# Two recurrences in one turn, three in the last: a two-pass expert kernel laid out anew from turn 9 on

## What is computed

```
x = x + rwkv(layernorm(x))          # time mix with the WKV recurrence, then channel mix
x = x + experts(layernorm(x))       # 8 experts, top 2, on a batch of tokens
x = x + recurrent(layernorm(x))     # h = a*h + scale*(i*conv(x)); out = rms(h @ W_out) * gamma
x = x + experts(layernorm(x))
# rwkv: k, v, r = mixes of x and its shift times w_key, w_value, w_recept
#       out = wkv(exp(decay), first, k, v) * sigmoid(r) @ w_output; x = x + out
#       vk = square(relu(mix @ f_w_key)) @ f_w_value; x = x + sigmoid(mix @ f_w_recept) * vk
# recurrent: depthwise conv of 4 taps; r, i = sigmoid(conv @ W); a = sigmoid(log_a)**(8*r)
#       scale = sqrt(1 - a*a)
# experts: h = gelu(x[tok] @ w1[e]); y = h @ w2[e]; out[tok] += y * weight, plus bias
```

## Time and profile before

| | us |
|---|---|
| median of three runs | 1547.81 |
| the profiled execution | 1548.36 |
| its span | 1546.6 |
| TensorE busy in it | 1278.7 (83%) |
| VectorE busy | 981.9 (63%) |
| ScalarE busy | 750.1 (48%) |
| GpSimd busy | 666.0 (43%) |

### The profile page before, as it was taken

The page is one execution under the profiler, slowest core; times in us unless marked ns, Lnnn a source line. Parts: engine busy times, 40 slices in busy tenths (PEclk is TensorE's granted clock), DMA queues, the critical chain, the costliest instruction groups (busy, mean ns, idle before and its releaser), DMA issues.

```text
span 1546.6 us, 17067 instructions
## 1 busy us (share of the span) xinstructions
PE 1278.7 (83%) x6050; PEld 1028.8 (67%) x6050; DVE 981.9 (63%) x1476; ACT 750.1 (48%) x1125; POOL 666.0 (43%) x529
## 2 busy tenths in 40 slices
PE   3398688999999999999777777799999989977641
PEld 1275557787778778777656565678778778866531
DVE  6787675557656675766889897956675746132334
ACT  2364254554736455464636363636455463534431
POOL 5323743255362535526565535462435523123161
PEclk9699889999999999999899989899999999998765
DMA  5000033335243333423001000143333425353321
GB/s 159 14 15 1 14 93 129 126 97 166 75 147 114 101 120 122 150 62 93 23 28 41 1 0 27 65 139 121 103 120 122 136 65 170 107 176 97 97 72 41
DMA packets 98372, 137.29 MB, mean 89 GB/s; under 512 B 9000, under 2 KB 83752, under 8 KB 98280
## 3 DMA queue, kind: packets, MB, share of 16 engines
q1 hardware_dynamic: 87408, 119.93, 24.3%
q0 software_dynamic: 4256, 10.24, 2.4%
q10 hardware_dynamic: 6624, 6.03, 1.1%
HBM read 119.64 MB, written 16.54 MB: 88 GB/s over the span
## 4 chain that ended last, share of the span: by engine, by line
PE 56%; DVE 13%; ACT 8%; issue 6%; POOL 4%; DMA 1%; ACTq 0%; POOLq 0%; DVEq 0%
PE psum L905 12%; PE psum L1033 10%; PE psum L1041 9%; PE psum L912 8%; PE psum L989 8%; PE psum L899 6%; PE psum L894 2%; DVE space L1347 2%; POOL xhat L432 1%; ACT dec L641 1%; POOL rstd L428 1%; DVE stats L1217 1%; ACT L792 1%; DVE kc L1308 1%; DVE dec L1310 1%
## 5 line engine op out<-in xcount | busy, mean ns | idle before, releaser
L428 POOL TENSOR_TENSOR rstd<-varis,half_neg 128x4 f32<-128x4 f32 (+1 forms) x48 | 76.8, 1600 | 483.7 <-DVE varis L1232 308.7
L989 PE MATMUL psum<-fwv,hid 128*128 128x256 f32 x1024 | 241.0, 382 | 0.8
L989 PEld LDWEIGHTS psum<-fwv,hid 128*128 128x128 f32 x1024 | 195.9, 192 | 33.7 <-ACT hid L659 3.4
L1033 PEld LDWEIGHTS psum<-xst,ew 128*128 128x128 f32 x1472 | 182.5, 198 | 42.5 <-ACT xst L720 23.5
L1033 PE MATMUL psum<-xst,ew 128*128 128x128 f32 x1472 | 188.1, 283 | 26.1 <-ACT xst L720 18.4
L1041 PE MATMUL psum<-ew,hidt 128*128 128x256 f32 x736 | 169.5, 384 | 4.4 <-ACT hidt L724 4.4
L1041 PEld LDWEIGHTS psum<-ew,hidt 128*128 128x128 f32 x736 | 141.0, 192 | 29.3 <-ACT hidt L724 5.7
L894 PE MATMUL psum<-ident,xhat 128*128 128x128 f32 x384 | 58.4, 302 | 98.8 <-POOL xhat L432 92.2
L894 PEld LDWEIGHTS psum<-ident,xhat 128*128 128x128 f32 x384 | 49.7, 157 | 108.7 <-POOL xhat L432 78.8
L655 ACT ACTIVATE hid<-psum 128x512 f32<-128x512 f32 x128 | 75.3, 597 | 95.3 <-PE psum L905 95.2
L525 POOL DMA_INDIRECT xs<-xf_rows,token_of_slot x46 | 55.8, 1212 | 142.8 <-PE psum L1021 120.3
(11 more groups left out here) (170 smaller groups left out, 2818.0 us busy)
## 6 DMA issues: line engine op xcount, KB each, us to landing
ew<-in_w SPq DMA_DIRECT2D x92, 1024.0 KB, 5.6
rows_ring<-in_x SPq DMA_DIRECT2D x14, 512.0 KB, 5.1
out<-rows_ring SPq DMA_DIRECT2D x14, 512.0 KB, 7.5
ys_rows<-ys ACTq DMA_DIRECT2D x46, 128.0 KB, 4.8
xf_rows<-ew SPq DMA_DIRECT2D x2, 1024.0 KB, 4.4
xf<-in_x SPq DMA_DIRECT2D x2, 512.0 KB, 4.5
space<-in_f_w_key SPq DMA_DIRECT2D x1, 1024.0 KB, 7.5
fwv<-in_f_w_value SPq DMA_DIRECT2D x1, 1024.0 KB, 10.3
```

The costliest lines, as they stand in the source:

```text
L428: pool.tensor_tensor(dst, src, half_neg[:, 0:src.shape[1]], ALU.pow).then_inc(done, 1)
L989: last = nc.tensor.matmul(rows4[:, k, :], hid[:, j % NHID, k * P:(k + 1) * P], fwv[:, j, :], start=j == 0 and k % 2 == 0, stop=j == FC - 1 ...
L1033: last = nc.tensor.matmul(bank_e[:, j * P:(j + 1) * P], ew1[:, c, at:at + P], xst[:, c, :], start=c == 0, stop=c == DC - 1)
```

## The change

`REC_TURN` now says in which turn each place's recurrence runs: places 0 to 5 in turns 4 to 9 as before, 6 and 7 in turn 10, 8 to 12 in turns 11 to 15, and 13, 14 and 15 in turn 16, the last. The turns 9, 10, 11 and 16 have orders of their own on each engine:

- Turn 9 (`turn_ahead`): both batches of pass one are picked and merged (their bias was added in turn 4), and the rows of places 6 and 7 are normalised. The second mix of batch 9 moves from the head of turn 10 to here.
- Turn 10 (`double_turn`): place 6 whole, and place 7 up to its convolution and split.
- Turn 11 (`turn_behind`): place 7 from its gates on, the experts' normalisation of pass two, then place 8 whole, and two tiles of pass two.
- Turns 12 to 15: four tiles each, as turns 13 to 16 had.
- Turn 16 (`tail`): the channel mix of batch 15, places 13 to 15 interleaved, five tiles, then the picks, the merge and the stores. Gated input, scaled input and residual of these places are on VectorE instead of GpSimd, and the last place's power on ScalarE as Ln and Exp.

There are two sets of recurrence buffers, of which the second (places 13 and 15) lies over the time mix's buffers, which are free by then. The scan's output and `fo` lie over `rg`. The normalised rows of place 7 lie in `hidt`, those of place 14 in the second row buffer. Semaphores are split so that steps of two places can be counted apart (`decays_made`, `root`, `gin_b`, `rec_om`), and waits on a shared PSUM bank stand in the order (`freed`) and no longer in the steps. Left out below: renamed waits, the helpers that say which set or row buffer a place has, ScalarE's orders of turns 10 and 11, TensorE's of turn 10, and the loops that call the new functions. The turn functions stand in this order: GpSimd, ScalarE, TensorE, VectorE.

```diff
 ORDER = [2, 3, 4, 5, 6, 7, 0, 1, 8, 9, 10, 11, 12, 13, 14, 15]
-REC0 = 4
-TURNS = range(-1, REC0 + B)
-MERGE = {9: 0, 10: 1}
+REC_TURN = [4, 5, 6, 7, 8, 9, 10, 10, 11, 12, 13, 14, 15, 16, 16, 16]
+DOUBLE = 10
+TAIL = 16
+TURNS = range(-1, TAIL + 1)
+MERGE_TURN = 9
 NX = 6
 NHID = 3
 
 
+SECOND_SET = (13, 15)
+HAT_IN_HIDDEN = 7
+HAT_IN_MIDDLE = 14
+SWAPPED = (8, 12)
...
-          12: "cd", 13: "abcd", 14: "abcd", 15: "abcd", 16: "abcd", 17: "acd", 18: "ac"}
+          11: "cd", 12: "abcd", 13: "abcd", 14: "abcd", 15: "abcd", 16: "abcde"}
...
+            fo = rg.rearrange("p a (b n) -> p (a b) n", n=D)
...
+        rec_hat = [xhat[0], xhat[1], hidt[:].rearrange("p (c a) n -> p c (a n)", c=TC)]
...
+            def turn_ahead(i, p):
+                norm1(i + 1)
+                keep3(p)
+                for b in range(NB):
+                    picking(0, b)
+                gated_input(p)
+                scaled_input(p)
+                norm2(i)
+                keep2(i)
+                mean_power(p)
+                residual(p)
+                norm3(p + 1)
+                norm3(p + 2)
+                keep1(i + 1)
+            def double_turn(i, p, q):
+                norm1(i + 1)
+                gated_input(p)
+                scaled_input(p)
+                norm2(i)
+                keep2(i)
+                mean_power(p)
+                residual(p)
+                keep1(i + 1)
+            def turn_behind(i, q, p):
+                gated_input(q)
+                scaled_input(q)
+                norm1(i + 1)
+                mean_power(q)
+                residual(q)
+                norm_power(1)
+                norm3(p)
+                keep3(p)
+                norm2(i)
+                gather(NT)
+                gather(NT + 1)
+                keep2(i)
+                next_gather(i, "c")
+                gated_input(p)
+                scaled_input(p)
+                next_gather(i, "d")
+                norm3(p + 1)
+                mean_power(p)
+                residual(p)
+                keep1(i + 1)
+            def tail():
+                mean_power(12)
+                residual(12)
+                next_gather(TAIL, "a")
+                norm3(14)
+                for p in (13, 14):
+                    keep3(p)
+                next_gather(TAIL, "b")
+                norm3(15)
+                keep3(15)
+                mean_power(13)
+                next_gather(TAIL, "c")
+                mean_power(14)
+                for b in range(NB):
+                    picking(1, b)
...
+            def tail():
+                b15 = B - 1
+                a, b, c, d, e = (TILE_AT[TAIL, place] for place in "abcde")
+                conv_in(13)
+                tile_columns(a)
+                nc.scalar.preload_act_table_set(GELU_TANH)
+                relu_of(b15, 0)
+                gelu_of(a, 0)
+                relu_of(b15, 1)
+                square_of(b15, 0)
+                gelu_of(a, 1)
+                receptance(b15)
+                relu_of(b15, 2)
+                square_of(b15, 1)
+                conv_in(14)
+                rows_back(a)
+                relu_of(b15, 3)
+                square_of(b15, 2)
+                relu_of(b15, 4)
+                square_of(b15, 3)
+                square_of(b15, 4)
+                decay_gates_out(13)
+                input_gates_out(13)
+                tile_columns(b)
+                blocks(b15, (5,))
+                nc.scalar.preload_act_table_set(LOG_EXP)
+                decays(13)
+                blocks(b15, (6,))
+                root_of(13)
+                blocks(b15, (7,))
+                nc.scalar.preload_act_table_set(GELU_TANH)
+                gelu_of(b, 0)
+                gelu_of(b, 1)
+                sums_of_squares(13)
+                decay_gates_out(14)
+                input_gates_out(14)
+                nc.scalar.preload_act_table_set(LOG_EXP)
+                decays(14)
+                conv_in(15)
+                root_of(14)
+                rows_back(b)
+                tile_columns(c)
+                nc.scalar.preload_act_table_set(GELU_TANH)
+                gelu_of(c, 0)
+                gelu_of(c, 1)
+                sums_of_squares(14)
+                decay_gates_out(15)
+                input_gates_out(15)
+                nc.scalar.preload_act_table_set(LOG_EXP)
+                decays(15)
+                rows_back(c)
+                tile_columns(d)
+                root_of(15)
+                nc.scalar.preload_act_table_set(GELU_TANH)
+                gelu_of(d, 0)
+                gelu_of(d, 1)
+                rows_back(d)
+                sums_of_squares(15)
+                tile_columns(e)
+                await_step(act, fin, 15, "ms")
+                nc.scalar.preload_act_table_set(LOG_EXP)
+                nc.scalar.activation(rms[:], msq[:], ACT.Ln).then_inc(last_pow.sem, 1)
+                act.wait_ge(last_pow.sem, last_pow.count(0, "ln"))
+                nc.scalar.activation(rms[:], rms[:], ACT.Exp, scale=-0.5).then_inc(last_pow.sem, 1)
+                nc.scalar.preload_act_table_set(GELU_TANH)
+                gelu_of(e, 0)
+                gelu_of(e, 1)
+                rows_back(e)
...
+            def turn_behind(i, q, p):
+                c, d = (TILE_AT[i, place] for place in "cd")
+                gate_products(q, [(relu, i - 2, "f7"), (kvr_out, i, "k0"), (kvr_out, i, "k1")])
+                value_columns(i)
+                recept_columns(i)
+                channel_key(i - 1, 0)
+                channel_key(i - 1, 1)
+                freed(fin, q - 1, f"f{TC - 1}")
+                receptances(i - 1)
+                channel_key(i - 1, 2)
+                channel_value(i - 1, 0)
+                channel_key(i - 1, 3)
+                channel_value(i - 1, 1)
+                channel_key(i - 1, 4)
+                channel_value(i - 1, 2)
+                freed(fr_out, i - 1, "s")
+                transposes_in(i + 1)
+                channel_key(i - 1, 5)
+                channel_value(i - 1, 3)
+                freed(ev1, i + 1, "e1")
+                rec_products(q)
+                for j in range(6, FC):
+                    channel_key(i - 1, j)
+                    channel_value(i - 1, j - 2)
+                channel_value(i - 1, FC - 2)
+                channel_value(i - 1, FC - 1)
+                freed(fin, q, f"f{TC - 1}")
+                outputs(i)
+                freed(zsum, i, "z")
+                transposes_rec(p)
+                tile_in(c)
+                freed(ev3, p, "c1")
+                transposes_mid(i)
+                tile_up(c, 0)
+                gate_products(p, [(relu, i - 1, f"f{j}") for j in (7, 5, 6)])
+                tile_up(c, 1)
+                keys(i + 1)
+                tile_down(c)
+                tile_in(d)
+                tile_up(d, 0)
+                freed(ev2, i, "e1")
+                rec_products(p)
+                tile_up(d, 1)
+                tile_down(d)
+            def tail():
+                b15 = B - 1
+                a, b, c, d, e = (TILE_AT[TAIL, place] for place in "abcde")
+                tile_in(a)
+                freed(ev2, b15, "e1")
+                freed(fin, 12, f"f{TC - 1}")
+                transposes_rec(13)
+                channel_key(b15, 0)
+                tile_up(a, 0)
+                channel_key(b15, 1)
+                freed(ev3, 13, "c1")
+                receptances(b15)
+                tile_up(a, 1)
+                channel_key(b15, 2)
+                channel_value(b15, 0)
+                tile_down(a)
+                freed(fr_out, b15, "s")
+                transposes_rec(14)
+                channel_key(b15, 3)
+                channel_value(b15, 1)
+                channel_key(b15, 4)
+                channel_value(b15, 2)
+                gate_products(13, [(relu, b15, f"f{j}") for j in (2, 3, 4)])
+                tile_in(b)
+                channel_key(b15, 5, 13)
+                channel_value(b15, 3)
+                channel_key(b15, 6, 13)
+                channel_value(b15, 4)
+                channel_key(b15, 7, 13)
+                channel_value(b15, 5)
+                channel_value(b15, 6)
+                channel_value(b15, 7)
+                tile_up(b, 0)
+                tile_up(b, 1)
+                freed(ev3, 14, "c1")
+                rec_products(13)
+                gate_products(14, [(relu, b15, f"f{j}") for j in (7, 5, 6)])
+                freed(fin, 13, f"f{TC - 1}")
+                transposes_rec(15)
+                tile_down(b)
+                tile_in(c)
+                tile_up(c, 0)
+                tile_up(c, 1)
+                freed(ev3, 15, "c1")
+                rec_products(14)
+                gate_products(15, [(gates_out, 14, "i1"), (gates_out, 14, "r1"), (gates_out, 14, "i0")])
+                tile_down(c)
+                tile_in(d)
+                tile_up(d, 0)
+                tile_up(d, 1)
+                tile_down(d)
```

(127 more changed lines are left out.)

734 lines of the change are left out of this document (456 added, 278 removed).

## The result

The changed kernel takes **1511.58 us** (median of four runs, 1510.34 to 1512.04) against 1548.45 for the kernel before on the same chip: a ratio of 0.9761, 95% interval 0.9744 to 0.9777. The prediction was 1503 with a range of 1470 to 1533. The span of the profiled execution is 1509.9 us where the prediction had 1502.

What follows compares the result with a forecast made beforehand. Bounds: TensorE in four-tile turns, nearly VectorE in turns 9 to 11, latency chains in the last turns. Sum: 1339.7 through turn 15, 122.8, 36.5, 3 for contention, span 1502; plus 1.2 gives 1503 us, range 1470 to 1533.

Steps and rivals of the forecast that it cites:

- The term for turn 16: Last turn up to the last copy: interleaved places and five tiles, tile e at +119, 122.8 us with the clock allowance.
- 4 for the clock: Turn 16: 4 us added for a lower TensorE clock in the gaps.
- Serial last turn: Rival: the three recurrences of turn 16 don't overlap, so it takes 184.6 us and the kernel 1565; chance 5%.
- Turn 10: From VectorE's weight scan of turn 10 to that of turn 11: 72.3 us, including place 7's taps and split.
- Turn 11: From VectorE's scan of turn 11 to the first tile of turn 12: 107 us, laid end to end.
- Contention: Turns 11 and 16: 3 us added because their layouts use undisturbed durations, while scale steps lengthen beside other engines' work.
- Turn 9: VectorE's weight scan of turn 9 to that of turn 10: 80.0 us before, net +0.5, mark at 806.8.
- The end: After tile e: copy, store, sixteen bare picks, last merge and output store, 36.5 us.
- Turns 12 to 15: Four tiles, mix, channel and one place each, like turns 13 to 15 before: 267.3 + 86.4 us.
- Perfect cover: Rival: turns 9 to 11 take 199 us instead of 263, or half that gain arrives: 1439 to 1470; chance 9%.
- Partly serial: Rival: turns 11 and 16 stand still 30 to 48 us more than laid out: 1533 to 1551; chance 5%.

Runs made afterwards that it cites:

- e1: The changed kernel run again with no edit, beside the edited kernels on the same chip: 1507.81 us, ratio 0.9744.
- e6: Changed kernel with VectorE's taps, split and gated input of places 14 and 15 put after the residual of the place before: 1541.17 us, ratio 0.9951.
- e2: Changed kernel with VectorE's `finish` of place 6 moved behind combine and the second mix in turn 10: 1507.17 us, ratio 0.9728.
- e4: Changed kernel with GpSimd's gathers of tiles c and d issued ahead of the second norm in turn 11: 1507.13 us, ratio 0.9741.
- e3: Changed kernel with the edit of e2 and, in turn 11, the quotient ahead of `finish` of place 7: 1505.21 us, ratio 0.9720.
- e5: Changed kernel with the edits of e3 and e4 together: 1501.93 us, ratio 0.9699.
- e9: Changed kernel with VectorE's taps and split of place 7 moved behind `finish` of place 6 in turn 10: 1514.31 us, ratio 0.9781.
- e10: Changed kernel with ten unread filler products on TensorE in turn 10, before second-norm transposes and place 6's products: 1511.13 us, ratio 0.9756.

## Why the prediction was right, and where it was off

**The sign and the size** came from the last turns, and that step held. The term for turn 16 was followed through four queues and said 118.8 and 4 for the clock. In e1, where tile d's down half keeps the full clock, the turn takes 119.2; in the changed kernel's profile 122.7. That both terms fit so closely is partly luck: the lower clock comes in either execution, and what it costs depends on whether it falls on a wait. The places inside it hold too: tile b's down half ends at +65.7 (forecast +66: 1419.12 + 3.62 less 1357.0), tile c waits 4.08 us behind ScalarE's copy ("about 5"), tile d ends at +103 and place 15's products at +107 in e1 (1454.76 + 3.72, 1458.32 + 3.62, from its start of turn 16 at 1355.2; forecast +103 and +106). The forecast that TensorE waits in this turn at most three times for over 5 us held: the longest wait is those 4.08.

**Serial last turn**, the slower rival, was turned down because taps, gated input and split of the next place stand ahead of this place's scan. e6 is that reason taken away, in VectorE's order alone: +30.6 us (+34.1 against e1), and TensorE twice waits 12 to 14 us for exactly these splits. The reason was the right one, the price of 184.6 us was not: with VectorE's order serial the turn takes 153.3, and even then the kernel is not slower than before (0.9951).

**Turn 10 (72.3 forecast, 82.0).** The step that failed is taking the distances of the earlier trace rows "with the waits that lie in it" and adding place 7's taps as if nothing else moved. `finish` of place 6 follows products that TensorE runs late and largely at the half clock, and VectorE stands 9.26 us in front of it. e2 shows that this one position is the whole 9.6 us between the marks of turn 10. It is not 9.6 us of time: most of it comes back behind the mark, as a wait of 7.82 us for TensorE, so a forecast by VectorE's marks alone was too narrow a measure.

**Turn 11 (107, 116.4).** The step was a plain sum "laid end to end" of 76, 9 and some 20, which make 105 and not the 107 that stand there. e4 puts 3.6 us of the excess down to a gather queued behind a norm that it does not need, of the kind the prediction asked about for the picks and did not ask for tiles c and d. e3 puts 3.1 on the place of `finish` of place 7. Between the scan of turn 10 and turn 12, where 179.3 was forecast, e5 still takes 188.8; what the last 9.5 us are I have not separated. Long scale steps (GpSimd's for the third norm of place 8 takes 5.77 us beside VectorE), TensorE's waits for `y` and for the scan of place 8 (11.56 and 4.93 us in e5) and VectorE's wait of 7.83 us for TensorE behind its weight scan lie there.

**Contention: +3 forecast.** It is not where I put it: turn 16 came to its sum, and turn 10, which the term did not name, has scale steps of 5.61 and 5.96 us where one alone takes 2.16. No run takes contention away altogether, so what it costs in all is not measured. In the prediction a rule of the Trainium skill stood beside the row: SBUF — State Buffer, "SBUF: two separate sides", a VectorE step with two SBUF inputs and a GpSimd step reading SBUF shut each other out for a whole instruction. By that rule the two take the sum of their times, and the runs agree nearly: scale step 2.16 alone and taps 4.07 alone (turn 16) make 6.2, and beside each other they span 5.6; in e9 taps, residual (2.00 at its shortest) and scale step make 8.2, and span 7.5 (870.02 to 877.50). The other rule, of the Trainium skill, ScalarE: Activation LUTs, "What ACT_TABLE_LOAD costs", asks for a drain of 1.38 us for each switch. This is a switch of turn 16 in the changed kernel, on ScalarE's timeline:

```profile
1469.57 1.28 ACT L1171 ACT_TABLE_LOAD   x1
1470.86 0.21 ACT L1172 ACTIVATE rms<-msq 128x4 f32<-128x4 f32 x1
```

The next step begins 0.01 us after the load, the load itself begins 0.01 us behind the step before it (1469.18 + 0.38), and the turn came to the sum without the drain. The measurement decides for 1.28.

**Turn 9.** The net +0.5 from scan to scan was -6.0 (74.0 for 80.0): one set of row statistics went ahead of the scan (728.1 to 730.6) and not behind it, and the scan of turn 9 comes 4.4 us later for that, a short wait and 1.2 us of drift. That is 2.5 of the 6.5 us. Of the rest some 2 are standstill (between the scans VectorE idles 12.4 us before and 7.2 now, where the forecast took off 3 to 4) and some 2 are work (busy 67.6 and 66.8, where the forecast had 4 more); I have not taken these apart further. The sixteen picks on GpSimd cost nothing that can be seen: the gated input starts right behind the last of them (767.5), and the scan of the place (773.7) does not wait for it. The two together leave -2.1.

**The end (36.5, 30.1).** The mechanism was right (bare picks, one after another); every size was a little high. Copy and store until the first pick take 2.4 us, not 5.2. The 4.8 for the store is in no row; it is the median of all 46 such stores in part 6 of the page before (the last number, us from issue to landing):

```profile
ys_rows<-ys ACTq DMA_DIRECT2D x46, 128.0 KB, 4.8
```

The last store alone lets the first pick start 2.0 us after its copy. Picks 19.8 (20.5), landing and last merge 2.8 (4), output store 5.2 (7, where the two times given, 1539.1 and 1546.6, are 7.5 apart). The five terms written there make 36.7 and not 36.5. This error and that of turn 10 are of opposite sign, and that is luck: without it I would have been 14 us low instead of 8.

**Turns 12 to 15** were 353.9 for 353.7: turns like them in the trace of before were the best measure there was.

**The other rivals.** Perfect cover had 199 us for turns 9 to 11 and the forecast 263; they take 278.7 (724.4 to 1003.1). Partly serial wanted 30 to 48 us more in turns 11 and 16 than laid out; they have 9.3 more.

## What to carry to other kernels

A turn with an order written by hand is worth laying out queue by queue; what decides is whether the next item's preparation stands ahead of this item's last wait on the same engine (here 30.6 to 34.1 us). When steps from a second item are put into a turn, look first at each step that waits at the head of an in-order queue, and at each DMA issue that stands behind a computation it doesn't need: three lines moved gave 9.6 us more between the marks. A removed standstill pays only up to the next late thing (9.6 us gained on VectorE gave 3.5), and a filled or quickened engine that waits for others pays nothing (e10), so measure between marks and not on the whole time.
